# Edge aggregation: message weights moved to ScalarE, in-degrees from a column of ones, attention histogram on VectorE

## The reference

```python
def _hconv(x, src, dst, ew, w1, b1, w2, b2, g, b):
    h = jax.nn.relu(x @ w1 + b1)
    msg = ew[:, None] * h[src]
    agg = jax.ops.segment_sum(msg, dst, num_segments=x.shape[0])
    h = agg @ w2 + b2
    return jax.nn.relu(_bn(h, g, b))
...
in_deg = jnp.minimum(jax.ops.segment_sum(ones, dst, num_segments=num_nodes), MAX_IN_DEGREE - 1)
```

## Time and profile before

| | us |
|---|---|
| median of 3 runs | 6274.06 |
| lowest and highest | 6262.47, 6277.19 |
| span of the profiled execution | 6224.7 |
| median less that span | 49.4 |
| first aggregation, first to last gather | 441.1 to 1581.4 |
| second aggregation's last gather, last addition | 3007.0, 3033.1 |

### The profile page before, as it was taken

The page is one execution under the profiler, slowest core; times in us unless marked ns, Lnnn a source line. Parts: engine busy times, 40 slices in busy tenths (PEclk is TensorE's granted clock), DMA queues, the critical chain, the costliest instruction groups (busy, mean ns, idle before and its releaser), DMA issues. The chain is left out here.

```text
span 6224.7 us, 73410 instructions
## 1 busy us (share of the span) xinstructions
PE 3894.4 (63%) x17328; PEld 2978.0 (48%) x17328; DVE 3162.7 (51%) x8327; ACT 2366.6 (38%) x6680; POOL 4026.6 (65%) x3591
## 2 busy tenths in 40 slices
PE   5645555555654555555756329987775877777763
PEld 4543343433453343333445228875554655556542
DVE  5544444444614444444578776535472435544566
ACT  2225566656425665666444213333441111111112
POOL 4876666666576666666588767875666666666523
PEclk7757777777776777777856569998997888889886
DMA  9774333333373333333378747868552112212235
GB/s 246 142 155 134 90 91 91 90 90 92 69 145 90 92 90 90 91 91 91 67 150 169 187 113 161 172 111 249 125 119 76 39 39 49 54 35 56 53 128 168
DMA packets 699733, 683.06 MB, mean 110 GB/s; under 512 B 96160, under 2 KB 623742, under 8 KB 698644
## 3 DMA queue, kind: packets, MB, share of 16 engines
q0 software_dynamic: 243744, 307.67, 25.2%
q1 hardware_dynamic: 440688, 345.82, 18.3%
q10 hardware_dynamic: 14980, 25.87, 1.2%
HBM read 475.03 MB, written 203.98 MB: 109 GB/s over the span
## 5 line engine op out<-in xcount | busy, mean ns | idle before, releaser
L729 POOL DMA_INDIRECT a_msg<-h_d,conv_src x1564 | 1479.0, 946 | 812.2 <-issue 437.0
L779 PE MATMUL a_part<-a_msg,a_pick 128*128 x3328 | 1226.9, 527 | 1046.6 <-issue 608.4
L621 POOL DMA_INDIRECT sums_d<-ss_total,ss_row_i x784 | 1276.5, 1628 | 452.1 <-issue 282.9
L779 PEld LDWEIGHTS a_part<-a_msg,a_pick 128*128 128x128 f32 x3328 | 819.5, 264 | 1415.1 <-issue 1271.6
L756 DVE TENSOR_TENSOR acc<-acc,a_part 128x256 f32 x1664 | 700.4, 421 | 1255.1 <-PE a_part L779 621.9
L3631 POOL DMA_INDIRECT es_edge<-gat_rows_d,el_idx x824 | 802.7, 974 | 473.4 <-issue 223.8
L743 DVE TENSOR_SCALAR a_pick<-ramp,conv_rel,conv_weight 128x128 f32<-128x128 f32 x1680 | 581.2, 347 | 0.2
L2581 ACT ACTIVATE cb_lent<-e_hp,e_b1c 128x256 f32<-128x256 f32 (+1 forms) x400 | 154.6, 469 | 1008.4 <-DMA gm_x<-in_L_gnn_z_out,gm_out_i 497.4
L2621 PE MATMUL e_yp<-cb_lent 128*128 128x256 f32 (+1 forms) x1568 | 417.0, 426 | 51.0 <-ACTq L2583 45.1
L2621 PEld LDWEIGHTS e_yp<-cb_lent 128*128 128x128 f32 (+1 forms) x1568 | 344.1, 221 | 116.7 <-ACTq L2583 47.1
L828 ACT ACTIVATE a1c_one_lo<-ramp,a1c_digits 128x128 bf16<-128x128 f32 x928 | 278.0, 387 | 311.0 <-remote 310.4
(11 more groups left out here) (557 smaller groups left out, 6851.0 us busy)
## 6 DMA issues: line engine op xcount, KB each, us to landing
ss_key_row<-keys_d SPq DMA_DIRECT2D x98, 512.0 KB
ss_pay<-in_edge_attr SPq DMA_DIRECT2D x97, 512.0 KB
a_msg<-h_d,conv_src POOLq DMA_INDIRECT x1564
experts_d<-cb_lent SPq DMA_DIRECT2D x96, 256.0 KB
cb_lent<-experts_d SPq DMA_DIRECT2D x30, 512.0 KB
y_rows_d<-node_h SPq DMA_DIRECT2D x28, 512.0 KB
e_xs<-y_rows_d SPq DMA_DIRECT2D x56, 256.0 KB
out_rows_d<-e_ys SPq DMA_DIRECT2D x56, 256.0 KB
```

Source lines behind the costliest of these rows:

```text
L621: nc.gpsimd.indirect_dma_start(self.out_d[q], bass.IndirectOffsetOnAxis(ap=self.row_i[n % 4][:, j:j + 1], axis=0), self.total[n % 4][:, j, ...
L729: nc.gpsimd.indirect_dma_start(msg[:, ds((j + PART) % SLOTS * C, C)], None, table, bass.IndirectOffsetOnAxis(ap=src_i[:, j:j + 1], axis=0) ...
L779: nc.tensor.matmul(part[b % BANKS][:, 0:C], pick[s % AHEAD][:], msg[:, ds(slot, C)], start=True, stop=True).then_inc(summed, 1)
```

## The change

ACT no longer makes one-hots. It takes each message row from its slot to a row buffer (six of them, 260 wide), times the edges' weights, and counts `weighted`; it loads the 26 registers that PE loaded. Columns 256 to 259 of the row buffers hold 1.0, so a product with an unweighted pick and 257 columns also counts edges by node; `acc` gets 260 columns, and column 256 is copied to in_deg after the first aggregation. PE has no registers left. SP frees a part when its rows are weighted, and does so three parts behind the part that it waits for. Only the attention's list is still counted, eight columns a window over both aggregations (128 batches); DVE makes its one-hots by two comparisons with a digit as scalar, in the first eight steps of a window. The destinations' digit lists are gone, and the digit lists are float32.

```diff
--- before.py
+++ after.py
@@ -30,6 +30,7 @@
 SLOTS = 32
+CW = 260
...
@@ -226,19 +226,6 @@
-
-    def list_dst_digits(self, dve):
-
-        nc, (lo, hi) = self.nc, self.dst_digits
-        nc.vector.memset(lo[:, CE:NS], 200.0)
-        nc.vector.memset(hi[:, CE:NS], 0.0)
-        nc.vector.tensor_copy(self.key_i[:], self.dst_cols[:])
-        dve.drain()
-        for listed, op, by in ((hi, ALU.logical_shift_right, 7), (lo, ALU.bitwise_and, 127)):
-            nc.vector.tensor_scalar(self.key_digit[:], self.key_i[:], by, None, op)
-            dve.drain()
-            nc.vector.tensor_copy(listed[:, 0:CE], self.key_digit[:])
...
@@ -394,8 +381,8 @@
-                nc.vector.tensor_scalar(self.tile_row[:, 0:4 * P], ends[0:1, 0, :], float(C), None, ALU.mult)
-                nc.vector.tensor_scalar(self.tile_row[:, 4 * P:NSB * P], ends[0:1, 1, 0:(NSB - 4) * P], float(C), None,
...
@@ -446,7 +433,7 @@
-    return [ctx.enter_context(k.nc.sbuf_tensor(f"{tag}_{n}", [P, chunks], BF16)) for n in ("lo", "hi")]
+    return [ctx.enter_context(k.nc.sbuf_tensor(f"{tag}_{n}", [P, chunks], F32)) for n in ("lo", "hi")]
...
@@ -664,11 +651,12 @@
     BANKS = 7
     K = 13
-    W = 4
     AHEAD = 8
+    ROWS = 6
     WINDOWS = NS // K
     PARTS = CE // PART
     RING = SLOTS // PART
+    BEHIND = 3
     V = 14
...
@@ -678,20 +666,15 @@
         msg = sb("msg", [P, SLOTS * C])
+        row = [sb(f"row{b}", [P, CW]) for b in range(ROWS)]
-        pick_ready = sem("pick_ready")
+        pick_ready, ones_made = sem("pick_ready"), sem("ones_made")
-        landed, freed = sem("landed"), sem("freed")
+        landed, weighted, freed = sem("landed"), sem("weighted"), sem("freed")
...
@@ -703,22 +686,35 @@
                 clear.start(sp)
             regs = [sp.alloc_register(f"{tag}_freed{v}") for v in range(V)]
             for p in range(PARTS):
-                if p % V == 1 and p <= PARTS - RING:
-                    sp.reg_load(regs, freed_row[0:1, p - 1:p - 1 + V])
-                    steps = [sp.snap(r, min_val=PART, max_val=NS) for r in regs]
                 sp.wait_ge(gathered[p % RING], 16 * sum(len(chunks(q)) for q in range(p % RING, p + 1, RING)))
                 sp.sem_inc(landed, 1)
-                if 0 < p <= PARTS - RING:
-                    sp.wait_ge(summed, steps[(p - 1) % V] & 1023)
+                old = p - BEHIND
+                if 0 <= old < PARTS - RING:
+                    if old % V == 0:
+                        sp.reg_load(regs, freed_row[0:1, old:old + V])
+                        steps = [sp.snap(r, min_val=PART, max_val=NS) for r in regs]
+                    sp.wait_ge(weighted, steps[old % V] & 1023)
                     sp.sem_inc(freed, 1)
             if clear:
                 clear.end(sp)
 
         @block.scalar
         def _(act):
-            def window(n, i, h):
-                counts.scalar_batch(act, h % 2, i * 2 + h // 2)
-            over_windows(act, W, window)
+            regs = [act.alloc_register(f"{tag}_{what}{b}") for b in range(K) for what in ("slot", "in")]
+            act.sem_inc(summed, ROWS)
+
+            def window(n):
+                act.reg_load(regs, chunk_row[0:1, ds(n * K, K), :])
+                slots = [act.snap(r, min_val=0, max_val=(SLOTS - 1) * C) for r in regs[0::2]]
+                parts = [act.snap(r, min_val=1, max_val=PARTS) for r in regs[1::2]]
+                for b in range(K):
+                    s = n * K + b
+                    act.wait_ge(landed, parts[b] & 255)
+                    act.wait_ge(summed, s + 1)
+                    nc.scalar.activation(row[s % ROWS][:, 0:C], msg[:, ds(slots[b], C)], ACT.Copy,
+                                         scale=weight[:, s:s + 1]).then_inc(weighted, 1)
+            for n in range(WINDOWS):
+                window(n)
 
         @block.gpsimd
         def _(pool):
...
@@ -733,6 +729,9 @@
         @block.vector
         def _(dve):
             counts.vector_start(dve)
+            for b in range(ROWS):
+                done = nc.vector.memset(row[b][:, C:CW], 1.0)
+            done.then_inc(ones_made, 1)
             nc.vector.memset(acc[:], 0.0)
             dve.drain()
...
@@ -740,132 +739,115 @@
 
             def make_pick(s, slot):
 
-                nc.vector.tensor_scalar(pick[slot][:], k.ramp[:], rel[:, ds(s, 1)], weight[:, ds(s, 1)],
-                                        ALU.is_equal, ALU.mult).then_inc(pick_ready, 1)
+                nc.vector.tensor_scalar(pick[slot][:], k.ramp[:], rel[:, ds(s, 1)], None, ALU.is_equal
+                                        ).then_inc(pick_ready, 1)
 
             for b in range(AHEAD):
                 make_pick(b, b)
 
             def window(n, i, h):
                 dve.reg_load(regs, first_row[0:1, ds(n * K, K)])
-                at = [dve.snap(r, min_val=0, max_val=(REAL_T - 1) * C) for r in regs]
+                at = [dve.snap(r, min_val=0, max_val=(REAL_T - 1) * CW) for r in regs]
                 for b in range(K):
                     s = n * K + b
-                    dve.wait_ge(summed, s + 1)
+                    dve.wait_ge(summed, ROWS + s + 1)
                     dve.wait_ge(added, s + R)
-                    nc.vector.tensor_tensor(sums[:, ds(at[b], C)], sums[:, ds(at[b], C)], part[b % BANKS][:, 0:C],
-                                            ALU.add).then_inc(added, 1)
+                    nc.vector.tensor_tensor(sums[:, ds(at[b], C + 1)], sums[:, ds(at[b], C + 1)],
+                                            part[b % BANKS][:, 0:C + 1], ALU.add).then_inc(added, 1)
                     make_pick(s + AHEAD, s % AHEAD)
+                    if b < counts.cols:
+                        counts.vector_column(dve, n, b)
             for n in range(WINDOWS):
                 window(n, n // 2, n % 2)
             counts.vector_end(dve)
+            if not first_batch:
+                dve.drain()
+                nc.vector.tensor_copy(in_deg[:, 0:NT], acc[:, :, C])
 
         @block.tensor
         def _(pe):
             pe.sem_inc(added, R)
             counts.tensor_start(pe)
-            regs = [pe.alloc_register(f"{tag}_{what}{b}") for b in range(K) for what in ("slot", "in")]
-
-            def window(n, i, h):
-                pe.reg_load(regs, chunk_row[0:1, ds(n * K, K), :])
-                slots = [pe.snap(r, min_val=0, max_val=(SLOTS - 1) * C) for r in regs[0::2]]
-                parts = [pe.snap(r, min_val=1, max_val=PARTS) for r in regs[1::2]]
+            pe.wait_ge(ones_made, 1)
+            for n in range(WINDOWS):
                 for b in range(K):
                     s = n * K + b
-                    pe.wait_ge(landed, parts[b] & 255)
-                    slot = slots[b]
+                    pe.wait_ge(weighted, s + 1)
                     pe.wait_ge(pick_ready, s + 1)
                     pe.wait_ge(added, s + 1)
-                    nc.tensor.matmul(part[b % BANKS][:, 0:C], pick[s % AHEAD][:], msg[:, ds(slot, C)], start=True, stop=True
-                                     ).then_inc(summed, 1)
-                counts.tensor_batch(pe, h % 2, i * 2 + h // 2)
-            for n in range(WINDOWS):
-                window(n, n // W, n % W)
+                    nc.tensor.matmul(part[b % BANKS][:, 0:C + 1], pick[s % AHEAD][:], row[s % ROWS][:, 0:C + 1],
+                                     start=True, stop=True).then_inc(summed, 1)
+                counts.tensor_batch(pe, n)
             counts.tensor_end(pe)
...
 class CountBeside:
-    BATCHES = 64
+    BATCHES = 128
...
-    def scalar_batch(self, act, q, n):
-
-        nc, B, digits = self.nc, self.cols[q], self.digits[q]
-        one = (self.one_lo[q], self.one_hi[q])
-        for a in (0, 1):
-            nc.scalar.copy(digits[:, a, :], self.kinds[q][a][:, ds((n + self.first) * B, B)])
-        act.drain()
-        act.wait_ge(self.used[q], n + 1)
-        for a in (0, 1):
-            for j in range(B):
-                nc.scalar.activation(one[a][:, j, :], self.k.ramp[:, 0:one[a].shape[2]], ACT.Square,
-                                     bias=digits[:, a, j:j + 1], scale=-1.0)
-        act.drain()
-        for a in (0, 1):
-            whole = one[a][:].rearrange("p b n -> p (b n)")
-            nc.scalar.activation(whole, whole, ACT.Relu, bias=self.k.ones[:, 0:1], scale=-1.0)
-        act.drain().then_inc(self.made[q], 1)
+    def vector_column(self, dve, n, j):
+
+        if j == 0:
+            dve.wait_ge(self.used, n + 1)
+        for one, listed in zip((self.one_lo, self.one_hi), self.lists):
+            at = (n + self.first) * self.cols + j
+            self.nc.vector.tensor_scalar(one[:, j, :], self.k.ramp[:, 0:one.shape[2]], listed[:, at:at + 1], None,
+                                         ALU.is_equal).then_inc(self.made, 1)
 
...
-    def tensor_batch(self, pe, q, n):
...
+    def tensor_batch(self, pe, n):
+
+        pe.wait_ge(self.made, 2 * self.cols * (n + 1))
+        for j in range(self.cols):
```

(58 more changed lines are left out.)

24 lines of the change are left out of this document (13 added, 11 removed).

## The result

The changed kernel takes 6399.73 us (median of 4 runs, 6397.76 to 6423.87), the kernel before 6273.41 us (4 runs). The ratio is 1.0197, 95% interval 1.0172 to 1.0223: slower by 126 us, where 6375 was forecast.

A forecast was written before the change was run, and what follows sets the result against it. Bound: POOL's gathers plus dry waits, 1.175 + 2.5/13 = 1.367 us a step. Dry time 0.8 us longer, 0.8/13 x 1664 steps = +102 us on 6274.1, gives 6376, rounded to 6375; range 6060 to 6500.

The forecast's parts named there:

- bound of 978 us an aggregation: POOL's gathers in an aggregation: 782 gathers, 1.25 us each from start to start, give a floor of 978 us.
- 325 us lost to dry waits: POOL out of free slots, waiting on SP's freeing line: 325 us really lost over both aggregations, 2.5 us a window.
- C: Rows on ACT join the aggregations' chain where SP waits for `weighted`, lengthening POOL's dry waits: slower, 6375 us, chance 0.46.
- +0.8: POOL's dry wait in each cycle: two missing rows at 0.40 us add 0.8 us, from a range of 0 to 1.9.
- n = 13: Steps in one cycle of the aggregations between dry waits, taken as 13 from a range of 11 to 14.
- the next part needs rows that ACT can only write once the late count frees row buffers: SP's freeing of parts: when a late count comes, none to four rows are missing, 0 to 1.9 us.
- The counts are late.: In the aggregations, PE's finished steps are counted late, only once gathers have paused, so POOL runs dry.
- ACT's 10.91 us: Reading at the second aggregation's start: ACT's next operation came 10.91 us late, cited as evidence that gathers are to blame.
- DVE: DVE's window work: one-hots at 0.280 and 0.255 us, thinning its burst to 0.88 us a step, at most 0.95.
- ACT's row: ACT's scaled copy of a message row: 0.397 to 0.474 us, the lower taken, 5.2 us a window.
- Rival A: In the aggregations, PE relieved of loads and register waits makes late counts rarer: faster, 6112 to 5949 us, chance 0.37.
- Rival D: DVE's 29 one-scalar operations a window hold up POOL's gathers: slower, +260 us on top, 6534 us, chance 0.04.

The follow-up runs named there:

- gathers_spaced: The kernel before with three semaphore counts of POOL's own behind each gather; 0.9998 of the kernel before on chip D.
- act_counts: The changed kernel with two semaphore counts of ACT's own behind each row; 1.0014 of the kernel before on chip E.
- weights_on_dve_2: The changed kernel with weights back in DVE's pick, PE loading registers and reading slots, SP one part behind, in-degrees not counted; 1.0056 of the kernel before, chip C.
- one_hots_apart_2: The changed kernel with DVE's one-hots and their PE products moved behind an aggregation's windows; 1.0923 of the kernel before on chip C.
- hots_batched: The changed kernel with a window's one-hots made by two two-input DVE operations instead of 16; 1.0125 of the kernel before on chip E.

## Why the prediction was right, and where it was not

- **The floor and the pauses.** The bound of 978 us an aggregation and the 325 us lost to dry waits were right. gathers_spaced on chip D, whose time is that of the kernel before (0.9998), ran at 986 and 978, 314 us less than chip A's 2277 for both.
- **The direction and the size.** C, slower by 102 us through longer dry waits, was likeliest; measured are 126 us. The pauses were forecast at 460 us and came to 468.7 us. On chips D and E there are no dry waits to lengthen, and near relatives of the change cost 0.2% and 0.1%: the forecast holds for chips with slow stretches, which the profile of before came from.
- **The terms of that sum.** Two were off and one made up for the other, which is luck. A dry wait beyond the usual distance grew from 2.61 us in the mean (324/124) to 3.24 (457/141), +0.63 and not +0.8. And a cycle holds 1664/141 = 11.8 steps, not 13: n = 13 was the wrong choice from the range of 11 to 14. By the prediction's own formula, 1.175 + 3.24/11.8 = 1.450 a step gives 2412 us for both aggregations; 2415 were measured. The additions behind the last gathers, 17 us more in the traces, were not in the sum.
- **The place.** The step "the next part needs rows that ACT can only write once the late count frees row buffers" failed: with half the buffers the time is the same. What the runs show in its place is that moving slots, registers and waits to ACT lengthens the pauses: 432.0 us against 349.7 on chip C, and 88 us (within 29) of the 122 to 154 that the change costs. The slow instructions on ACT (35 ns to 1.4 us) fit this, but that they are the cause was not shown; the run meant to test it, act_counts, fell on a chip without them. It stays open.
- **"The counts are late."** This was half of it. In the slow stretches single instructions that wait for nothing take 0.7 to 1.4 us, on PE, ACT, POOL and SP. The prediction took it for a matter of semaphores alone, though its own reading of ACT's 10.91 us pointed to more.
- **DVE.** The one-hots at 0.281 and 0.248 us (0.280 and 0.255 forecast) and a step of 0.89 us (905.72 to 906.61 in the trace; 0.88 forecast) were right. Of their share, 34 us, some 19 lie behind the last gathers (against chip A's trace of before), where the prediction counted nothing.
- **ACT's row.** 0.495 us, at the upper row's 0.474 rather than the 0.397 taken. It changed nothing: rows followed each other every 0.40 us.
- **Rival A**, that PE relieved thins out the pauses, got 0.37. With PE at 8 histogram products a window and ACT idle (weights_on_dve_2) the gathers took 1144 and 1139 us. With PE free of registers and of all products beside (one_hots_apart_2) they took 1186 and 1181. Neither relief of PE made the pauses rarer or shorter; PE without registers was only run with ACT bearing them.
- **Rival D** did not happen in the change: gathers at 948 ns in the mean, 1.139 us at most, beside 29 one-scalar operations a window. By the rule in the Trainium skill, "SBUF — State Buffer", section "Who interferes with whom", tensor-scalar operations could have blocked POOL; this trace shows hardly anything of it. The two-input form in hots_batched does. What the change's trace shows is the other direction. Of its 1680 picks 159 take over 400 ns, up to 533, all of them begun 0.47 us or more after the start of a gather and ended within 0.13 us of its end:

```profile
1294.68 0.95 POOL L725 DMA_INDIRECT a_msg<-h_d,conv_src  x1 [0.30 <-issue]
...
1295.15 0.53 DVE L742 TENSOR_SCALAR a_pick<-ramp,conv_rel 128x128 f32<-128x128 f32 x1
```

## What to carry to other kernels

A wait that returns every window, tied to a pause of another engine, is a circle, and its price is pauses times length: count both in the trace before costing a change, as a stage added inside the circle changes both. Moving work to an idle engine isn't free when that engine then carries the waits and registers of the chain. And before a difference of some per cent is worked on, run the kernel on several chips and compare its simplest instruction.

## What the runs showed of the hardware that was not expected

- The same kernel took 6216 to 6273 us on three chips and 5532 to 5539 us on two. In both aggregations the median distance of two gathers is 1.25 us on all five, but for the run with drains; on the three chips alone there are stretches in which a register operation takes 700 to 1400 ns instead of 32 to 35. They were seen only beside dense gathers, and seldom in the first 9 us after a pause of POOL. Why one chip has them and another not stays open.
- A drain of POOL behind an indirect gather of 128 rows of 1 KB costs some 2.27 us: the median distance of two gathers goes from 1.25 to 3.52 us.
- Up to five semaphore counts behind a gather cost nothing where no stretch is slow, as three left the distance at 1.251 us and five in the quick stretches of chip C too.
- A DVE comparison with two inputs in SBUF, 128x1024, beside a gather: 1.85 us for the gather instead of 0.95.
- No version here beats the kernel before on either kind of chip. What the slow stretches leave to win is the difference of the two kinds: 314 us between first and last gathers of the two aggregations and 35 us behind them (kernel before on A, gathers_spaced on D), and about as much again in stages that the change doesn't touch, the attention's gathers above all (1275 us on A, 1066 on D).
